# Moving one ScalarE copy (the values) ahead of four exponentials and two gelus in a fused attention and feed-forward pipeline

## The chip, the core and the metric

The kernel runs on one core of a Trainium2 chip. The core has a matrix engine (TensorE, PE in the profile; its weight loads stand apart as PEld), VectorE (DVE), ScalarE (ACT), GpSimd (POOL) and SyncE (SP), which here issues all the DMAs. Each engine works through its own instructions in the order in which they were written, and waits on semaphores for the others. The metric is the device time of one execution in microseconds (us), smaller being better. Everything is in 32-bit floats.

## The reference

The input is 4 sequences of 1024 tokens with 128 features. After a layernorm, 8 blocks of linear attention with a feed-forward part run over it (the first stage). After a second layernorm follow 6 layers of local attention with 16 heads of 64 features and windows of 32 tokens, each with a gated feed-forward part (the second stage). The change lies in the second stage, whose layer is

```
def attn_layer(x, Wqkv, qs, ksc, Wo):
    q, k, v = jnp.split(x @ Wqkv, 3, -1)          # 16 heads of 64 each
    q = l2norm(q) * qs;  k = l2norm(k) * ksc
    q = rotate(q);  k = rotate(k)                 # cos/sin tables with a scale
    out = local_attention(q, k, v)                # scores, mask, softmax, times v
    return out @ Wo                               # own window of 32 and the one before
def ffn_layer(x, g, bln, W1, b1, W2, b2):
    hg = layernorm(x, g, bln) @ W1 + b1
    a, gate = jnp.split(hg, 2, -1)                # 341 features each
    return a * jax.nn.gelu(gate, approximate=False) @ W2 + b2
for i in range(6):
    x = attn_layer(shift_tokens(x), ...) + x
    x = ffn_layer(shift_tokens(x), ...) + x
```

## The kernel before, in words

The second stage is a software pipeline over 192 tiles (6 layers of 32 tiles, 128 tokens each). Every engine has a loop `for s in range(-3, TILES + LAG)`, and each pass, here a step, does different parts of the work for different tiles: the products for tile s + 1 or s, the exponentials for tile s - 1, the product of probabilities and values for tile s - 3. The feed-forward part works on chunks of four tiles, with a lag of 8 to 11 steps, so the steps come in groups of four. In this document a group's steps are named by what the chunk does in them:

- step D (lag 8): TensorE turns the chunk (`ff_turn`), VectorE takes its statistics, ScalarE normalizes it (`ff_unit`, L974);
- step A (lag 9): TensorE turns it back (`ff_back`), ScalarE scales it (`ff_norm`, L982);
- step B (lag 10): three gate products (`ff_gate`, L783) and three value products (`ff_value`, L791) on TensorE, three gelus on ScalarE (`ff_gelu`, L988), three products `ff_hidden` on VectorE (L1278);
- step C (lag 11): TensorE's last feed-forward product (`ff_down`, L798).

In time the order is A, B, C, D, A and so on. 46 chunks have their step B in a step in which `values` runs too (the chunk's lag of 10 leaves the last two of 48 to the drain).

TensorE's order in a step is: keys (`keys_of`, L667), `attend` (L739), queries (L667), `turn_k` (L699), the chunk's turns, `output` (L748), `turn_q` (L699), `ff_down` in step C, values (`values_of`, L667), the first gate and value products in step B, `scores` (L720), the rest of the gate and value products in step B. The product of the values goes to the two banks `kv_ps`, where the keys of the next step go too: `keys_of` waits for `v_r`, which ScalarE's copy of the values (`values`, L969) counts up. `values_of` itself waits until VectorE has read the next tile's keys there. `turn_k` waits for GpSimd's `unit_k` (L497), `turn_q` for its `unit_q` (L503); between these two GpSimd does `probs_norm` (L490). All three wait for VectorE.

ScalarE's order in a step is: square of the keys (L930), `outputs` (L962), square of the queries (L930), `turned_k` (L941), eight exponentials (L954, one for each head, each with a read of its accumulator), `turned_q` (L946), four exponentials, two gelus in step B, `values` (L969), `ff_norm` in step A, `ff_unit` in step D, the third gelu in step B, the last four exponentials, and a small copy of keys (L935). Gelu and exponential are in different tables, so step B holds two loads of a table (ACT_TABLE_LOAD, 1.28 us each).

VectorE waits for the last exponential of tile s - 1 before it masks the scores of tile s (`masked`, L1240), since both use `sc`. Then come the reciprocal of the sums, the maxima, the rotation of the next keys, the transpose of the probabilities (L1255), and the rest of its step. In step B it takes the gelu's output from `gate`, a single buffer that the next gelu overwrites.

The program's order is the order written in the loops; no scheduler changes it.

Of the kernel before, what the change touches and what calls it, by code (L numbers as in the profile page):

```python
# [71 lines left out]
def build(nc, xT, wa1, wa2, wb, wf, rot, mask, outT):  # L72
    with ExitStack() as ctx:
# [129 lines left out]
        def live(t):  # L203

            return 0 <= t < TILES

        def chunk(s, lag):

            return (s - lag) // PER if (s - lag) % PER == 0 and 0 <= s - lag < TILES else None

        def need(eng, s, v):

            if v > 0:
                eng.wait_ge(s, v)
# [9 lines left out]
        def x_at(c):  # L224

            _, b, u = of(c)
            return slice(seq_col(b, COL * u), seq_col(b, COL * u) + COL)
# [300 lines left out]
        def _(pe):  # L528
# [21 lines left out]
            def first_matmul(bank, c, w, count):  # L550
                l, _, _ = of(c)
                pe.matmul(ps[:, bank, :], Wa1[l % 2][:, w * D:(w + 1) * D], X[:, x_at(c)], start=True, stop=True)\  # L552
                    .then_inc(count, 1)

            def query(c):
                l, _, _ = of(c)
                if c % NC == 0:
                    pe.wait_ge(la1[l % 2], 16 * (l // 2 + 1))
                x_in(pe, c)
                if c > 0:  # L560
                    pe.wait_ge(Q_r, c)
                first_matmul(Q_BANK, c, 0, qp_mm)
# [273 lines left out]
        def _(act):  # L836
# [51 lines left out]
            def ff_gelu(c):  # L888
                act.wait_ge(f2_mm, MA * c + 4)
                act.activation(g2[c % 2], ps[:, F2_BANK, :], ACT.Gelu_apprx_tanh, bias=vec(c, A2_BF2))\  # L890
                    .then_inc(g2_r, 1)
# [35 lines left out]
            def square(t, src, half, mm, count):  # L927
                act.wait_ge(mm, t + 1)
                need(act, red_r, t)
                act.activation(sq[:, half], src.rearrange("p b c -> p (b c)"), ACT.Square).then_inc(count, 1)  # L930

            def keys_on(t):

                need(act, s_mm, t)
                act.activation(kT[:, :, 0:WIN], kT[:, :, P:P + WIN], ACT.Copy,  # L935
                               scale=inside[:, t % TS:t % TS + 1]).then_inc(shift_r, 1)

            def turned_k(t):
                act.wait_ge(trk_mm, t + 1)
                act.wait_ge(shift_r, t + 1)  # L940
                act.activation(kT[:, :, WIN:WIN + P], s_ps.rearrange("p b (c t) -> p (b c) t", t=P),  # L941
                               ACT.Copy).then_inc(kT_r, 1)

            def turned_q(t):
                act.wait_ge(trq_mm, t + 1)
                act.activation(qTf, s_ps.rearrange("p b c -> p (b c)"), ACT.Copy).then_inc(qT_r, 1)  # L946

            def exponents(t, some):

                if some[0] == 0:  # L950
                    act.wait_ge(max_r, t + 1)
                    need(act, pt_r, t)
                for h in some:
                    i = act.activation(pe3[:, :, h, :], sc[:, 64 * h:64 * h + 64].rearrange("p (k q) -> p k q", k=2),  # L954
                                       ACT.Exp, bias=nmx[:, h:h + 1], accum_out=rs[:, h:h + 1])
                if some[-1] == HEADS - 1:
                    i.then_inc(exp_r, 1)

            def outputs(t):
                act.wait_ge(pv_mm, t + 1)  # L960
                need(act, wo_r, t)
                act.activation(OTf.rearrange("p (c r q) -> p r c q", r=2, q=WIN),  # L962
                               o_ps.rearrange("p r (c q) -> p r c q", q=WIN), ACT.Copy).then_inc(ot_r, 1)

            def values(t):

                act.wait_ge(v_mm, t + 1)
                need(act, vs_in, 32 * (t - 1))
                act.activation(vv[t % RING][:, 1, :], kv_ps.rearrange("p b c -> p (b c)"), ACT.Copy).then_inc(v_r, 1)  # L969

            def ff_unit(q):
                act.wait_ge(frs_r, 2 * q + 2)
                for j in range(PER):
                    i = act.activation(fx[:, j * P:(j + 1) * P], ps[:, FO_BANK, j * P:(j + 1) * P], ACT.Identity,  # L974
                                       bias=shift[:, j:j + 1], scale=rstd[:, 0, j:j + 1])
                i.then_inc(fn_r, 1)

            def ff_norm(q):
                if q % (NT // PER) == 0:
                    act.wait_ge(lf, 16 * (q * PER // NT + 1))  # L980
                act.wait_ge(fb_mm, q + 1)
                act.activation(fn, ps[:, FO_BANK, :], ACT.Identity, bias=WF[:, F_B:F_B + 1],  # L982
                               scale=WF[:, F_G:F_G + 1]).then_inc(xn_r, 1)
# [8 lines left out]
            for s in range(-3, TILES + LAG):  # L992
                if live(s + 1):
                    square(s + 1, kv_ps, K, k_mm, sqk_r)
                if live(s - 3):
                    outputs(s - 3)
                if live(s + 1):
                    square(s + 1, q_ps, Q, q_mm, sqq_r)
                if live(s):
                    turned_k(s)  # L1000
                if live(s - 1):
                    exponents(s - 1, range(0, 4))
                    exponents(s - 1, range(4, 8))
                if live(s):
                    turned_q(s)
                if live(s - 1):
                    exponents(s - 1, range(8, 12))
                if chunk(s, 10) is not None:
                    ff_gelu(chunk(s, 10), 0)
                    ff_gelu(chunk(s, 10), 1)  # L1010
                if live(s):
                    values(s)
                if chunk(s, 9) is not None:
                    ff_norm(chunk(s, 9))
                if chunk(s, 8) is not None:
                    ff_unit(chunk(s, 8))
                if chunk(s, 10) is not None:
                    ff_gelu(chunk(s, 10), 2)
                if live(s - 1):
                    exponents(s - 1, range(12, 16))  # L1020
                if 0 < s + 1 < TILES:
                    keys_on(s + 1)
# [380 lines left out]
```

## Time and profile before

| | us |
|---|---|
| median of 3 runs | 3965.4 (3961.76 to 3970.67) |
| the profiled execution | 3970.83 |
| its span in the profile | 3969.0 |

| engine | busy us | share of the span |
|---|---|---|
| PE (matmuls) | 3711.0 | 93% |
| DVE | 3427.1 | 86% |
| ACT | 3283.5 | 83% |
| POOL | 2394.3 | 60% |

The mean granted clock of TensorE is 0.981 of full speed. The second stage runs from about 915 us to the end, three quarters of the span. Busy time of TensorE includes time in which a matmul waits in the pipeline, so 93% doesn't say that it works at its peak. The share of an engine doesn't say either whether it is waited for: for this the waits and the order of events within a group of four steps have to be read.

### The profile page before, as it was taken

What the parts mean: (1) busy time and instruction counts of PE and PEld (TensorE: products, weight loads), DVE (VectorE), ACT (ScalarE), POOL (GpSimd) and SP (SyncE); (2) the same over time, 40 slices, a digit from 0 to 9 for tenths busy, and PEclk for the clock granted to TensorE, in tenths of its full rate; (3) what the DMA queues carried; (4) which work ended last, traced back from release to release, by engine and by line L of the source; (5) the groups of instructions that cost most, each with busy time, mean ns of one, the idle gap of its engine ahead of it and who ended that gap; (6) DMA issues with size and microseconds to landing.
All of it is one profiled execution on the core that took longest, in us unless ns stands there. A gap on an engine that the chain in (4) does not pass through costs nothing.

```text
span 3969.0 us, 124299 instructions
## 1 busy us (share of the span) xinstructions
PE 3711.0 (93%) x49248; PEld 2334.9 (59%) x49248; DVE 3427.1 (86%) x7048; ACT 3283.5 (83%) x9269; POOL 2394.3 (60%) x1468
## 2 busy tenths in 40 slices
PE   5999999976999999999999999999999999999996
PEld 2444444433666666666666666666666666666664
DVE  6999999957888988889888888988989889898894
ACT  3999999964888888888888888888888888888884
POOL 2444433435766767667676666766767667676672
PEclk7999999987999999999999999999999999999998
DMA  1000000001222323223232232322323223232321
GB/s 50 3 9 11 12 9 21 17 1 38 79 82 77 97 81 84 82 75 99 80 85 82 76 95 79 88 77 81 97 79 86 78 80 98 81 86 79 84 79 54
DMA packets 129599, 263.07 MB, mean 66 GB/s; under 512 B 34944, under 2 KB 36736, under 8 KB 128768
## 3 DMA queue, kind: packets, MB, share of 16 engines
q1 hardware_dynamic: 129024, 255.16, 23.0%
q8 instruction: 391, 6.41, 0.7%
q14 instruction: 184, 1.51, 0.1%
HBM read 26.43 MB, written 2.10 MB: 7 GB/s over the span
## 4 chain that ended last, share of the span: by engine, by line
PE 48%; ACT 23%; DVE 16%; issue 7%; POOL 4%; DMA 2%; SPq 2%; DVEq 0%; ACTq 0%; POOLq 0%
PE ps L667 12%; ACT arena L954 12%; PE ps L739 6%; PE ps L611 5%; PE ps L606 5%; PE ps L552 4%; PE ps L547 3%; ACT arena L941 3%; ACT arena L946 2%; DVE arena L1255 2%; DVE arena L1176 2%; PE ps L798 2%; DVE arena L1169 2%; DVE ssq L1197 2%; PE ps L748 2%
## 5 line engine op out<-in xcount | busy, mean ns | idle before, releaser
L954 ACT ACTIVATE arena<-arena,nmx 128x64 f32<-128x64 f32 x3072 | 1024.9, 340 | 42.3 <-DVE arena L1255 40.3
L497 POOL TENSOR_TENSOR arena<-arena,rinv 128x1024 f32<-128x1024 f32 x192 | 365.3, 1902 | 622.3 <-DVE rinv L1228 622.3
L667 PE MATMUL ps<-WB,arena 128*128 128x512 f32 x1152 | 572.4, 620 | 50.3 <-ACT arena L969 30.5
L667 PE MATMUL ps<-WN,arena 128*128 128x512 f32 x1152 | 560.1, 608 | 38.3 <-ACT arena L969 30.8
L954 ACT ACTIVATION_READ_ACCUMULATOR arena<-arena,nmx 128x1 f32 x3072 | 594.5, 194 | 0.0
L930 ACT ACTIVATE arena<-ps 128x1024 f32<-128x1024 f32 x384 | 392.1, 1021 | 227.6 <-PE ps L667 222.0
L481 POOL TENSOR_TENSOR arena<-arena 128x1024 f32<-128x1024 f32 x192 | 454.3, 2366 | 182.1 <-DVE arena L1169 162.1
L1176 DVE TENSOR_TENSOR arena<-ps,tables 128x512 f32<-128x512 f32 x768 | 490.1, 678 | 18.7 <-ACT arena L930 18.5
L486 POOL TENSOR_TENSOR arena<-arena 128x1024 f32<-128x1024 f32 x192 | 453.6, 2362 | 50.7 <-DVE arena L1169 47.1
L739 PEld LDWEIGHTS ps<-arena 128*64 128x64 f32 x12288 | 379.6, 139 | 164.2 <-issue 132.0
L1169 DVE TENSOR_TENSOR arena<-ps,tables 128x1024 f32<-128x1024 f32 x384 | 459.4, 1196 | 0.0
L1197 DVE TENSOR_REDUCE ssq<-arena 128x32 f32<-128x2048 f32 x192 | 435.2, 2267 | 0.0
L699 PEld LDWEIGHTS ps<-ident,arena 128*128 128x128 f32 x3072 | 353.8, 142 | 117.5 <-issue 102.7
L490 POOL TENSOR_TENSOR arena<-arena,rr 128x1024 f32<-128x1024 f32 x192 | 367.7, 1915 | 87.3 <-DVE rr L1249 87.3
L739 PE MATMUL ps<-arena 128*64 128x64 f32 x12288 | 405.4, 225 | 15.6 <-DMA arena<-arena 14.6
L699 PE MATMUL ps<-ident,arena 128*128 128x128 f32 x3072 | 399.9, 273 | 13.4 <-POOL arena L497 4.3
L720 PEld LDWEIGHTS ps<-arena 64*32 64x32 f32 x24576 | 265.4, 105 | 189.8 <-issue 188.2
L748 PE MATMUL ps<-arena,WB 128*128 128x128 f32 x3072 | 374.7, 275 | 2.2 <-ACT arena L962 1.1
L503 POOL TENSOR_TENSOR arena<-arena,rinv 128x1024 f32<-128x1024 f32 x192 | 370.0, 1927 | 0.0
L748 PEld LDWEIGHTS ps<-arena,WB 128*128 128x128 f32 x3072 | 358.1, 192 | 2.7 <-DMA WB<-wb 1.3
L443 POOL TENSOR_TENSOR rstdA<-veA,power 128x4 f32<-128x4 f32 x128 | 129.7, 1013 | 369.5 <-DVE veA L1129 369.5
L667 PEld LDWEIGHTS ps<-WB,arena 128*128 128x128 f32 x1152 | 202.9, 193 | 234.8 <-issue 211.9
(113 smaller groups left out, 7104.5 us busy)
## 6 DMA issues: line engine op xcount, KB each, us to landing
arena<-arena SPq DMA_DIRECT2D x1536, 64.0 KB
arena<-arena SPq DMA_DIRECT2D x192, 384.0 KB, 3.4
arena<-arena SPq DMA_DIRECT2D x192, 128.0 KB, 3.5
arena<-X SPq DMA_DIRECT2D x96, 128.0 KB, 3.1
arena<-Y SPq DMA_DIRECT2D x96, 128.0 KB, 3.1
WB<-wb SPq DMA_DIRECT2D x15, 512.0 KB, 5.8
arena<-wa SPq DMA_DIRECT2D x8, 581.0 KB, 3.7
WN<-wb SPq DMA_DIRECT2D x9, 512.0 KB, 4.6
```

The source lines that it names most:

```text
L481: pool.tensor_tensor(tu[:, K], t1[:, K], t2[:, K], ALU.add).then_inc(addk_r, 1)
L486: pool.tensor_tensor(tu[:, Q], t1[:, Q], t2[:, Q], ALU.add).then_inc(addq_r, 1)
L503: pool.tensor_tensor(heads(tu[:, Q]), heads(tu[:, Q]), wide(rinv[:, 0:HEADS], DH), ALU.mult).then_inc(q_r, 1)
L667: i = pe.matmul(banks[:, c, :], x, W[:, w * INNER + c * COL:w * INNER + (c + 1) * COL], start=True, stop=True)
L699: i = pe.transpose(s_ps[:, j // 4, (j % 4) * P:(j % 4 + 1) * P], src[:, j * P:(j + 1) * P], ident[:, :])
L739: i = pe.matmul(o_ps[64 * a:64 * a + 64, side, c * 64:(c + 1) * 64], vv[t % RING][:, side, h * DH:(h + 1) * DH], pw[:, side, :, a, c, :], ...
L748: i = pe.matmul(o_ps[:, 0, 0:P], WB[:, B_WO + c * D:B_WO + (c + 1) * D], OT[:, c, :], start=(c == 0), stop=(c == NP - 1))
L930: act.activation(sq[:, half], src.rearrange("p b c -> p (b c)"), ACT.Square).then_inc(count, 1)
L954: i = act.activation(pe3[:, :, h, :], sc[:, 64 * h:64 * h + 64].rearrange("p (k q) -> p k q", k=2), ACT.Exp, bias=nmx[:, h:h + 1], accum_o ...
L1169: dve.tensor_tensor(heads(t1[:, half]), src.rearrange("p b (h d) -> p (b h) d", d=DH), w, ALU.mult)\
L1176: k = dve.tensor_tensor(heads(t2[:, half])[:, :, here], src.rearrange("p b (h d) -> p (b h) d", d=DH)[:, :, there], w, ALU.mult)
L1197: dve.tensor_reduce(ssq[:, :], heads(sq), AX_X, ALU.add).then_inc(red_r, 1)
```

## The change

In ScalarE's loop, `values(s)` moves up by one or two places: it stood behind the third group of four exponentials and, in step B, behind two gelus. Now it stands directly behind `turned_q(s)`. Nothing else differs; the instructions, their sizes and their waits are the same.

```
                 if live(s):
                     turned_q(s)
+                    values(s)
                 if live(s - 1):
                     exponents(s - 1, range(8, 12))
                 if chunk(s, 10) is not None:
                     ff_gelu(chunk(s, 10), 0)
                     ff_gelu(chunk(s, 10), 1)
-                if live(s):
-                    values(s)
                 if chunk(s, 9) is not None:
                     ff_norm(chunk(s, 9))
```

The first place is ScalarE's step B, from `turned_q` (L946) on, before the change: the copy of the values is L969, the gelus are L988, the exponentials L954.

```order
L946 ACTIVATE arena<-ps 128x1024
L954 ACTIVATE arena,rs<-arena,nmx 128x2x32 x4
L988 ACT_TABLE_LOAD
L988 ACTIVATE arena<-ps,WF 128x512 x2
L969 ACTIVATE arena<-ps 128x1024
L988 ACTIVATE arena<-ps,WF 85x512
L954 ACT_TABLE_LOAD
L954 ACTIVATE arena,rs<-arena,nmx 128x2x32 x4
```

The same stretch of ScalarE's step B after the change.

```order
L946 ACTIVATE arena<-ps 128x1024
L969 ACTIVATE arena<-ps 128x1024
L954 ACTIVATE arena,rs<-arena,nmx 128x2x32 x4
L988 ACT_TABLE_LOAD
L988 ACTIVATE arena<-ps,WF 128x512 x2
L988 ACTIVATE arena<-ps,WF 85x512
L954 ACT_TABLE_LOAD
L954 ACTIVATE arena,rs<-arena,nmx 128x2x32 x4
```

The copy moved from between the second and the third gelu to a place ahead of the first table load, and the three gelus now follow one another.

The second place is ScalarE's step C, the one with no chunk work on this engine, from `turned_q` (L946) to the copy of keys (L935), before the change.

```order
L946 ACTIVATE arena<-ps 128x1024
L954 ACTIVATE arena,rs<-arena,nmx 128x2x32 x4
L969 ACTIVATE arena<-ps 128x1024
L954 ACTIVATE arena,rs<-arena,nmx 128x2x32 x4
L935 ACTIVATE arena<-arena,inside 128x8x32
```

The same stretch of step C after the change.

```order
L946 ACTIVATE arena<-ps 128x1024
L969 ACTIVATE arena<-ps 128x1024
L954 ACTIVATE arena,rs<-arena,nmx 128x2x32 x8
L935 ACTIVATE arena<-arena,inside 128x8x32
```

All eight of the remaining exponentials now stand behind the copy, where four stood before. The order on the other four engines is the same.

## Rows read from the trace of the kernel before

**Rows 1.** Waits of PE from 1000 to 3800 us: us in total, times, longest.

```profile
PE ps L667 <- ACT arena L969: 59.4, 90, 0.8
PE ps L783 <- ACT arena L988: 5.7, 35, 0.4
```

**Rows 2.** Waits of DVE from 1000 to 3800 us.

```profile
DVE arena L1278 <- ACT arena L988: 141.7, 82, 3.2
```

**Rows 3.** Timeline, step B: start, us, engine, line, xcount, [idle before <-releaser].

```profile
2017.58 1.01 ACT L946 ACTIVATE arena<-ps 128x1024 f32<-128x1024 f32 x1
...
2019.93 1.28 ACT L988 ACT_TABLE_LOAD   x1
...
2021.22 0.69 ACT L988 ACTIVATE arena<-ps,WF 128x512 f32<-128x512 f32 x1
2021.94 0.75 DVE L1278 SCALAR_TENSOR_TENSOR arena<-ps,WF,arena 128x512 f32<-128x512 f32 x1 [2.35 <-ACT arena L988]
...
2022.79 0.69 ACT L988 ACTIVATE arena<-ps,WF 128x512 f32<-128x512 f32 x1 [0.88 <-DVE arena L1278]
2023.37 1.02 ACT L969 ACTIVATE arena<-ps 128x1024 f32<-128x1024 f32 x1
...
2023.53 1.09 PE L783 MATMUL ps<-arena,WF 128*85 128x512 f32 x2 [0.16 <-ACT arena L988]
...
2024.66 0.68 ACT L988 ACTIVATE arena<-ps,WF 85x512 f32<-85x512 f32 x1 [0.27 <-PE ps L783]
...
2025.31 1.88 PE L667 MATMUL ps<-WB,arena 128*128 128x512 f32 x4
```

**Rows 4.** Timeline, the step C behind it.

```profile
2035.78 1.00 ACT L946 ACTIVATE arena<-ps 128x1024 f32<-128x1024 f32 x1
...
2037.07 1.88 PE L667 MATMUL ps<-WB,arena 128*128 128x512 f32 x4
...
2038.99 1.02 ACT L969 ACTIVATE arena<-ps 128x1024 f32<-128x1024 f32 x1 [0.88 <-PE ps L667]
...
2039.91 0.34 ACT L954 ACTIVATE arena<-arena,nmx 128x64 f32<-128x64 f32 x1
...
2041.23 0.50 ACT L935 ACTIVATE arena<-arena,inside 128x256 f32<-128x256 f32 x1
...
2041.43 1.22 DVE L1240 TENSOR_TENSOR arena<-ps,maskt 128x1024 f32<-128x1024 f32 x1
```

**Rows 5.** Busy time from C's masking to A's values: window, us, then each engine.

```profile
2041.43:2065.25 23.82, 23.06 (x350) 16.66 (x349) 23.09 (x41) 20.30 (x65) 19.38 (x11) 1.00 0.39 110
```

**Rows 6.** Timeline, the end of step D and step A.

```profile
2052.95 1.01 ACT L969 ACTIVATE arena<-ps 128x1024 f32<-128x1024 f32 x1
...
2053.86 1.49 ACT L974 ACTIVATE arena<-ps,shift,rstd 128x128 f32<-128x128 f32 x4
...
2054.11 1.96 PE L667 MATMUL ps<-WB,arena 128*128 128x512 f32 x4 [0.76 <-ACT arena L969]
...
2055.99 1.95 PEld L739 LDWEIGHTS ps<-arena 128*64 128x64 f32 x64 [0.76 <-ACT arena L974]
...
2056.84 1.90 POOL L497 TENSOR_TENSOR arena<-arena,rinv 128x1024 f32<-128x1024 f32 x1 [1.92 <-DVE rinv L1228]
...
2058.70 1.92 POOL L490 TENSOR_TENSOR arena<-arena,rr 128x1024 f32<-128x1024 f32 x1
...
2060.57 1.91 POOL L503 TENSOR_TENSOR arena<-arena,rinv 128x1024 f32<-128x1024 f32 x1
...
2062.82 0.91 PEld L699 LDWEIGHTS ps<-ident,arena 128*128 128x128 f32 x8
```

**Rows 7.** Timeline, from step A into an earlier step B.

```profile
2007.19 1.95 PE L667 MATMUL ps<-WB,arena 128*128 128x512 f32 x4 [0.68 <-ACT arena L969]
...
2012.50 1.91 POOL L503 TENSOR_TENSOR arena<-arena,rinv 128x1024 f32<-128x1024 f32 x1
...
2015.46 0.91 PEld L699 LDWEIGHTS ps<-ident,arena 128*128 128x128 f32 x8
```

More of the change, by code:

```diff
@@ L1005, in _ @@
                     turned_q(s)
+                    values(s)
                 if live(s - 1):
@@ L1010, in _ @@
                     ff_gelu(chunk(s, 10), 1)
-                if live(s):
-                    values(s)
                 if chunk(s, 9) is not None:
```

## The prediction

> **What bounds the kernel now.** I read the page's busy shares first (TensorE 93%, VectorE 86%, ScalarE 83%: no engine is far from full), then the waits of TensorE and VectorE, and then one whole group of four steps in the timeline, because the waits alone don't tell what is late next. The waits show the target of this change: over 2800 us TensorE stands still 90 times for the copy of the values, 59.4 us in all, 0.66 us a time [rows 1]. 2800 us hold about 45 groups, so it is two of the four steps. The timeline says which: the keys at the start of A (0.76 us, behind D) and at the start of B (0.68 us, behind A) [rows 6, 7]. Behind B and C the keys start without such a wait [rows 3]. The second thing to see is who else is near the edge. In step B VectorE idles 2.35 us for the first gelu, and TensorE starts its third gate product as soon as the second gelu ends, 0.16 us after it could have [rows 3]; over the whole stage TensorE waits there 35 times, but only 5.7 us [rows 1], so the two are level. From C's masking to A's values VectorE is busy 23.09 of 23.82 us, and TensorE 23.06 [rows 5]: two engines that run side by side, neither with room. VectorE's slack all lies in B, where it waits for gelus 141.7 us in all [rows 2].
>
> **The change, part by part.** No instruction is added or removed, so the working is in the places. The copy takes 0.91 us of ScalarE's queue (from its start at 2052.95 to the next instruction at 2053.86 [rows 6]). All is for one group of four steps, relative to before, positive being later.
>
> Steps D and A, the gain. The copy no longer stands behind four exponentials. D's turned queries end about 0.2 us before the product of the values is there, so the copy would run about 1 us earlier, and end before TensorE has finished the scores. Both waits of the keys go: up to 0.76 + 0.68 = 1.44 us a group, if nothing else is late.
>
> Step B, the first loss. ScalarE runs without a gap from the turned queries (2017.58) into the table load and the first gelu (2021.22) [rows 3]. The copy now stands in this chain, and its product is done by then, so that it doesn't wait: every gelu comes 0.91 us later. Before, the copy lay in a hole: between the second gelu and the third, ScalarE has to wait for TensorE's third gate product anyway, and even with the copy in it 0.27 us of that hole was left [rows 3]. So the cover is free and goes unused. The third gate product starts when the second gelu ends, the next keys behind it, and VectorE's three products wait for the gelus too. The slack is nil on TensorE (it already waits 0.16 us), and VectorE's idle 2.35 us grow instead of shrinking. TensorE and VectorE both enter C 0.91 us late.
>
> Step C, the second loss. Between the turned queries and the values TensorE does `ff_down` here. The turned queries end at 2036.78, the product of the values only lets ScalarE go on at 2038.99 [rows 4]. Before, four exponentials filled 1.32 us of this and 0.88 us were idle; now 2.2 us are idle, and the four exponentials come behind the copy. Four of them take 2041.23 - 2039.91 = 1.32 us [rows 4]. Queued behind the waiting copy are these, the last four, the copy of keys and the next square. VectorE's masking waits for the last exponential; it started at 2041.43 without a wait, some 0.10 us after that exponential, so it now starts 1.32 - 0.10 = 1.22 us later. VectorE is then 0.91 + 1.22 = 2.13 us late, TensorE 0.91. ScalarE itself has idle time soon after, and catches up.
>
> Steps D and A, what is late next. VectorE has no room here [rows 5], so it stays 2.13 us late; and it feeds GpSimd. In A, `unit_k` waits for VectorE, with `probs_norm` and `unit_q` right behind it [rows 6], so all three are 2.13 us late, and `unit_q` ends at 2060.57 + 1.91 + 2.13 = 2064.61. TensorE wanted to turn these queries at 2062.82 [rows 6]. It turns them 1.79 us late, whatever it gained at the start of A. Nor was all of that gain there: `attend` in A waits for ScalarE's `ff_unit`, 2055.99 [rows 6], which stands behind copy and exponentials as before and is 0.65 us late by the same working. From the turn to the scores all is 1.79 us late. The keys of B then start without their 0.68 us: 1.79 - 0.68 = 1.11 us a group later than before.
>
> Does it settle there? B's keys are 1.11 us late and VectorE 2.13, 1.02 us behind TensorE. In B `unit_q` ended at 2014.41 and the turn of the queries came at 2015.46 [rows 7]: 1.05 us of slack, which just holds 1.02. The 2.35 us in front of the first gelu then take up VectorE's lag, and the next group starts as this one did. So the loss is 1.11 us in each group.
>
> Other queues: SyncE shifts the values behind their copy, and waits for it (the eight issues for the probabilities, in front of it, are out by then), and the shifted values are used three steps later. The transposed probabilities of D are 2.1 us later, their DMAs too; by their issues in the trace they would land about a microsecond ahead of the `attend` that needs them. The table loads stay two a group, at 1.28 us [rows 3].
>
> **The sum.** 46 groups x 1.11 us = 51 us. The profiled execution took 3970.8 us, so its like would take 4022; it lay 5.4 us above the median of the runs, and against that median of 3965.4 the forecast is 4016 us, 1.3% slower. The parts not seen in a row are small: the 0.1 us between last exponential and masking could be 0 to 0.2; how far VectorE recovers between C and A is bounded by 0 and its idle 23.82 - 23.09 = 0.73 us [rows 5]. That gives 0.4 to 1.2 us a group, 3984 to 4021. Upwards, if DMAs or the 1.02 against 1.05 us of slack in B add up to 0.6 us, 4044.
>
> **The rivals.**
> 1. Both waits go and nothing comes back: 1.44 us x 46 = 66 us less, 3899. For it speaks only the list of waits, in which the copy is TensorE's largest wait for another engine [rows 1]. It would need slack behind the copy in B, and there is none [rows 3]. The Trainium skill (Perfetto Trace Analysis, Optimization Strategies) says that where the matmul engine is idle waiting for others, one should optimize the engines that block it; taken alone, this rule gives that time.
> 2. Faster, the other side: B costs its 0.91 us, both waits go, and VectorE's lag from C never reaches TensorE: 0.91 - 1.44 = -0.53 us x 46, 3941. The place is `unit_q` in A: it ends at 2062.48, 0.34 us before TensorE's turn [rows 6]. Faster comes out if VectorE is less than about 0.9 us late there; I have 2.13.
> 3. No change: C costs nothing (the masking isn't held), all engines carry B's 0.91 us, and A gains only down to `ff_unit`: 0.65 late at `attend`, less 0.68 at B's keys, nil. 3966.
> 4. Worse: the lags add up with nothing taken back, 0.91 + 1.22 = 2.13 us x 46 = 98 us, 4063. It would need the keys to keep waiting for their copy, which now comes about 1 us earlier.
>
> **How the numbers follow.** A measurement here tells 0.2%, about 8 us, from no change. Chances: forecast 0.71, rival 1 0.03, rival 2 0.09, rival 3 0.08, rival 4 0.09. Faster 0.12 (rivals 1 and 2), same 0.08, slower 0.80. The range from 3980 to 4050 holds the forecast's own spread and half of what lies between it and rival 4; the faster cases and rival 3 stay outside.
>
> **What would show it.** Right: TensorE's wait for the copy nearly gone; ScalarE's wait for the product of the values in front of L969 grown from 0.88 to 2.2 us in C; VectorE's wait for the gelus grown to above 3 us in B; TensorE's wait at the third gate product 0.9 us or more; a new wait of TensorE's turn for GpSimd's L503 in A; the group of four steps 1.1 us longer. Wrong: the masking in C at its old place relative to the keys (rival 3), or TensorE's turn in A without a wait for L503 (rival 2). What would upset all of it is a copy that waits long in B.

## The result and the profile after

| | before | after |
|---|---|---|
| median of the runs, us | 3966.6 (4 runs) | 4033.9 (4 runs, 4031.4 to 4037.8) |
| ratio of after to before | | 1.017 (95% interval 1.0157 to 1.0182) |
| span of the profiled execution, us | 3969.0 | 4034.4 |
| busy us PE, DVE, ACT, POOL | 3711.0, 3427.1, 3283.5, 2394.3 | 3730.8, 3424.8, 3283.4, 2395.2 |

The change makes the kernel slower by 67 us; forecast were 51, with a range of 3980 to 4050. The work of the engines is the same (ScalarE's busy time differs by 0.1 us); what grew is waiting. In the kernel after, VectorE's lines stand one lower: L1239 is the masking, L1254 the transpose, L1277 the product with the gate.

The waits of TensorE from 1000 to 3860 us (total, times, longest), to be held against [rows 1]:

```profile
PE ps L739 <- DMA arena<-arena: 49.6, 66, 1.3
PE ps L720 <- ACT arena L946: 22.6, 46, 0.8
PE ps L791 <- ACT arena L988: 19.5, 39, 0.6
PE ps L783 <- ACT arena L988: 19.5, 44, 0.7
...
PE ps L699 <- POOL arena L503: 11.8, 35, 0.8
```

The wait for the copy, 59.4 us before, is gone altogether. Five others are now large, 123 us together, where they were about 21 before. Two are for the gelus of step B, one is for GpSimd's `unit_q` in step A, as forecast. The first two, put down to DMAs and to the turned queries, were not.

The first row has to be taken apart before it can be used. `attend` waits for several things: the DMAs of its tile's probabilities, the DMAs that shift its tile's values (done 13 us before in the group below), VectorE's sum `Y` of the tile before, and in step A also ScalarE's `ff_unit`. The list names whichever of their semaphores moved last, even if the count that `attend` asks for had been reached long before. In step A of the group shown below (in the kernel after):

```profile
2070.25 0.59 SPq L354 DMA_DIRECT2D arena<-arena  x1
...
2072.36 1.48 ACT L974 ACTIVATE arena<-ps,shift,rstd 128x128 f32<-128x128 f32 x4
...
2073.84 0.27 DVE L1259 TENSOR_TENSOR Y<-ps,X 128x128 f32<-128x128 f32 x1
...
2074.38 2.08 PE L739 MATMUL ps<-arena 128*64 128x64 f32 x64 [0.81 <-DMA arena<-arena]
```

The last probability DMA landed 0.50 us before `attend` started, by its semaphore. VectorE's `Y` ended at 2074.11, 0.27 us before it, and this is what came last. The DMA that the row names is the shift of a later tile's values. Held against the counts that `attend` asks for, the row splits like this in each trace (us, times, 1000 to 3800 us; the rows for this window are within 0.1 us of the sums):

| | the tile's probability DMAs last (nearly all in step B) | `ff_unit` or `Y` last (all in step A) |
|---|---|---|
| before | 4.5, 13 | none |
| after | 21.4, 30 | 28.3, 36 |
| D and A early (e1 below) | 19.8, 29 | 14.1, 27 |
| D early (e10) | 4.0, 13 | 14.9, 28 |
| A early (e11) | 19.1, 26 | none |
| e1 with half of the DMAs (e6) | none | 16.2, 29 |
| after with half of the DMAs (e7) | none | 36.0, 38 |

So the DMAs really hold `attend` for 21 us after the change, not for 49.6. The part in step A was seen in the forecast, which named `ff_unit` for it; the part in step B was not.

Step B after the change in the timeline (start, us, engine, line, [idle before <-releaser]), against [rows 3]:

```profile
2038.10 1.28 ACT L988 ACT_TABLE_LOAD   x1
2039.40 0.69 ACT L988 ACTIVATE arena<-ps,WF 128x512 f32<-128x512 f32 x1
2040.12 0.75 DVE L1277 SCALAR_TENSOR_TENSOR arena<-ps,WF,arena 128x512 f32<-128x512 f32 x1 [3.01 <-ACT arena L988]
2040.14 1.12 PE L791 MATMUL ps<-arena,WF 128*128 128x512 f32 x2 [0.55 <-ACT arena L988]
2040.96 0.69 ACT L988 ACTIVATE arena<-ps,WF 128x512 f32<-128x512 f32 x1 [0.88 <-DVE arena L1277]
2041.70 1.09 PE L783 MATMUL ps<-arena,WF 128*85 128x512 f32 x2 [0.44 <-ACT arena L988]
2042.83 0.68 ACT L988 ACTIVATE arena<-ps,WF 85x512 f32<-85x512 f32 x1 [1.18 <-PE ps L783]
```

ScalarE's idle time before the third gelu grew from 0.27 to 1.18 us: by 0.91 us, the length of the copy that lay there. VectorE's wait for the first gelu grew from 2.35 to 3.01 us. TensorE's wait at the third gate product is 0.44 us, where 0.9 or more was forecast, since 0.55 us of it now fall on the second value product (L791), which also needs the first gelu. The two make 0.99 us.

From step C to the next step B, against [rows 4, 6, 7]:

```profile
2057.17 1.02 ACT L969 ACTIVATE arena<-ps 128x1024 f32<-128x1024 f32 x1 [2.21 <-PE ps L667]
2060.93 1.23 DVE L1239 TENSOR_TENSOR arena<-ps,maskt 128x1024 f32<-128x1024 f32 x1 [1.38 <-ACT arena L954]
...
2076.09 1.90 POOL L497 TENSOR_TENSOR arena<-arena,rinv 128x1024 f32<-128x1024 f32 x1 [1.92 <-DVE rinv L1227]
...
2081.23 0.35 ACT L954 ACTIVATE arena<-arena,nmx 128x64 f32<-128x64 f32 x1 [0.89 <-DVE arena L1254]
2081.77 1.09 PE L699 MATMUL ps<-ident,arena 128*128 128x128 f32 x8 [0.30 <-POOL arena L503]
...
2085.04 1.59 PE L720 MATMUL ps<-arena 64*32 64x64 f32 x128 [0.46 <-ACT arena L946]
2086.57 1.98 PE L667 MATMUL ps<-WB,arena 128*128 128x512 f32 x4
2089.03 2.09 PE L739 MATMUL ps<-arena 128*64 128x64 f32 x64 [0.48 <-DMA arena<-arena]
```

All of this is read against the first gelu of the group (2021.22 before, 2039.40 after). The copy in C waits 2.21 us, forecast 2.2. The masking comes 21.53 us behind the gelu, before 20.21: 1.32 us later, forecast 1.22. In A, `unit_k` is 1.07 us later, so VectorE made up 0.25 us on the way. TensorE turns the queries late and waits for GpSimd, as forecast. But ScalarE's exponentials in A now wait 0.89 us for VectorE's transpose, because they overwrite what it reads, so that the turned queries are late too, and the scores with them. Then B's `attend` waits 0.48 us for its DMAs, and here they do land last, 0.14 us before it starts.

How long is one group? The table load ahead of the first gelu marks each. In nearly every trace several groups have the same length within 0.03 us, which is also the shortest; these are the undisturbed ones. (The group of the timeline above is 62.68 us long, 0.56 above it, and 0.48 of this is B's wait for DMAs.) One before the change, from one such row to the next:

```profile
2582.86 1.28 ACT L988 ACT_TABLE_LOAD   x1
...
2643.71 1.28 ACT L988 ACT_TABLE_LOAD   x1
```

and after it:

```profile
2548.31 1.28 ACT L988 ACT_TABLE_LOAD   x1
...
2610.43 1.28 ACT L988 ACT_TABLE_LOAD   x1
```

60.85 against 62.12 us: 1.27 us a group, against 1.11 in the forecast. In the mean over 46 groups it is 67 / 46 = 1.46 us. The 46 lengths of each trace tell where: the 40 ordinary groups grew by 1.51 us in the mean, the five that hold a boundary of layers by 0.65, and the last, in the drain, by 1.67.

### The profile page after: what moved, and what is told of

Same layout as the page of the kernel before. It is cut to its first block, busy times and chain, and to the rows that moved or that the text cites. A ratio compares the mean times of both kernels' runs of the same rounds, so it can differ in the third digit from the quotient of the medians.

```text
span 4034.4 us, 124299 instructions
## 1 busy us (share of the span) xinstructions
PE 3730.8 (92%) x49248; PEld 2341.1 (58%) x49248; DVE 3424.8 (85%) x7048; ACT 3283.4 (81%) x9269; POOL 2395.2 (59%) x1468
## 3 DMA queue, kind: packets, MB, share of 16 engines
q14 instruction: 184, 1.51, 0.1%
## 4 chain that ended last, share of the span: by engine, by line
PE 47%; DVE 19%; ACT 17%; issue 7%; POOL 5%; SPq 3%; DMA 2%; DVEq 0%; ACTq 0%; POOLq 0%
PE ps L667 11%; ACT arena L954 8%; PE ps L611 5%; PE ps L739 5%; PE ps L606 5%; PE ps L552 4%; PE ps L547 3%; DVE arena L1175 3%; PE ps L798 3%; DVE arena L1254 3%; DVE arena L1168 2%; PE ps L748 2%; PE ps L699 2%; DVE ssq L1196 2%; ACT arena L969 2%
## 5 line engine op out<-in xcount | busy, mean ns | idle before, releaser
L954 ACT ACTIVATE arena<-arena,nmx 128x64 f32<-128x64 f32 x3072 | 1023.7, 339 | 72.6 <-DVE arena L1254 71.5
L954 ACT ACTIVATION_READ_ACCUMULATOR arena<-arena,nmx 128x1 f32 x3072 | 589.8, 192 | 0.0
L739 PEld LDWEIGHTS ps<-arena 128*64 128x64 f32 x12288 | 381.9, 139 | 214.7 <-issue 138.1
L739 PE MATMUL ps<-arena 128*64 128x64 f32 x12288 | 406.6, 225 | 62.9 <-DMA arena<-arena 61.9
L720 PEld LDWEIGHTS ps<-arena 64*32 64x32 f32 x24576 | 268.7, 105 | 204.6 <-issue 202.6
L503 POOL TENSOR_TENSOR arena<-arena,rinv 128x1024 f32<-128x1024 f32 x192 | 369.9, 1927 | 0.0
L1239 DVE TENSOR_TENSOR arena<-ps,maskt 128x1024 f32<-128x1024 f32 x192 | 234.9, 1223 | 149.2 <-ACT arena L954 140.3
```

The lines of the kernel that those rows point to most:

```text
L503: pool.tensor_tensor(heads(tu[:, Q]), heads(tu[:, Q]), wide(rinv[:, 0:HEADS], DH), ALU.mult).then_inc(q_r, 1)
L739: i = pe.matmul(o_ps[64 * a:64 * a + 64, side, c * 64:(c + 1) * 64], vv[t % RING][:, side, h * DH:(h + 1) * DH], pw[:, side, :, a, c, :], ...
```

## The experiments

Each ratio is to the kernel before, run on the same chip. In the kernels e1 to e4 and e8 to e12 the copy stands early in the steps that are named, and elsewhere as before. The edit of e1 is

```
                 if live(s):
                     turned_q(s)
+                if live(s) and s % 4 in (0, 1):
+                    values(s)
...
-                if live(s):
+                if live(s) and s % 4 not in (0, 1):
                     values(s)
```

where s % 4 is 0 in D, 1 in A, 2 in B and 3 in C. The others have another set: (0, 1, 2) for e2, (0, 1, 3) for e3, (3,) for e8, (2,) for e9, (0,) for e10, (1,) for e11.

**e1: D and A alone.**

> The copy of the values moves ahead only in steps D and A; B and C keep the old order. My theory: the two waits of TensorE for the copy vanish (1.44 us a group), but the gain is cut by what is level with them in the trace of before: in A the first exponentials wait for VectorE's transpose, which ends as the turned keys do, and the attend of B waits for DMAs that follow that transpose. What is left is 0.1 to 0.7 us a group, taken as 0.5: 46 x 0.5 = 23 us, 3943 us, ratio 0.994. Rival (the waits are worth what the list says): 1.44 x 46 = 66 us less, 3900. Rival (VectorE and its DMAs close the loop by themselves): 0.1 x 46, about 3961, no change.

Measured: 3957.7 us, ratio 0.9974 (0.9965 to 0.9984), so some 10 us or 0.22 us a group, of the 1.44 us in the list of waits. The rival that takes the list at its word is refuted. The sign and the cause of the cut are those of the theory, at the lower part of its 0.1 to 0.7 us. Where the waits went is plain in TensorE's waits from 1000 to 3800 us:

```profile
PE ps L739 <- DMA arena<-arena: 33.9, 56, 1.6
PE ps L720 <- ACT arena L946: 23.2, 48, 0.8
```

The 59.4 us of waits for the copy are down to 4.3, and these two rows have grown by 44.2 us together (before: 4.4 and 8.5). Of the 33.9 us, 19.8 are for the DMAs, nearly all in step B, and 14.1 are in step A, for `ff_unit` and `Y`. A row of its own, `PE ps L739 <- ACT arena L974`, holds another 5.0 us of that.

**e2: D, A and B (C as before).**

> As in the changed kernel, but step C keeps the old order, so that the four exponentials stand ahead of the copy there. My theory: B costs its 0.91 us, C nothing, D and A give about 0.5 us: +0.4 us a group, 46 x 0.4 = 18 us, 3985 us, ratio 1.005; VectorE's masking in C starts where it did before, relative to the gelus; TensorE's waits for DMAs and for GpSimd's L503 are gone again. Rival (C costs nothing, the whole loss is B's): as the changed kernel, 4034, 1.017. Rival (the saved waits count in full): 0.91 - 1.44, 3942.

Measured: 3996.6 us, ratio 1.0062 (1.0045 to 1.0079). The forecast for it was 1.005. C's order does cost something, and B's too: beside e1, B's early copy costs 0.0088, 35 us. In an undisturbed group the masking in C comes 21.51 us behind the table load, as before the change (22.83 in the kernel after), and the waits for L503 are back at 1.9 us (1.5 before), both as expected. The row of waits for DMAs isn't gone, as expected it would be, but 32.2 us.

**e3: D, A and C (B as before).**

> As in the changed kernel, but step B keeps the old order, with the copy between the second and the third gelu. My theory: B's 0.91 us go and all else stays as in the changed kernel: 1.46 - 0.91 = 0.55 us a group, 46 x 0.55 = 25 us, 3992 us, ratio 1.006; VectorE's wait for the gelus is back near 3.2 us a group, masking in C is 1.3 us late after the gelus. Rival (C costs nothing): as with D and A alone, 3943.

Measured: 3993.0 us, ratio 1.0063 (1.0046 to 1.0080), as forecast. Beside e1, C's early copy costs 35 us as well. VectorE's wait for the gelus (same stretch) is back near that of before (141.7), while its wait for exponentials stays as high as in the changed kernel (81.3 before, 128.3 after):

```profile
DVE arena L1242 <- ACT arena L954: 127.8, 132, 1.8
DVE arena L1280 <- ACT arena L988: 124.9, 75, 3.2
```

**e4: D and A early, and in B the copy between the first and the second gelu.**

```
                     ff_gelu(chunk(s, 10), 0)
+                    if live(s):
+                        values(s)
                     ff_gelu(chunk(s, 10), 1)
...
+                if live(s) and s % 4 not in (0, 1) and chunk(s, 10) is None:
+                    values(s)
```

> D and A as in e1, C old; in B the copy stands between the first and the second gelu, where ScalarE idles 0.88 us for VectorE anyway. My theory: the copy's 0.91 us fill that hole and delay the second gelu by 0.03 us, so the time is that of e1 within 0.05 us a group (2 us). Rival (any place ahead of the last gelu delays the gelu chain by the copy's 0.91 us): 42 us above e1.

Measured: 3953.9 us, ratio 0.9966 (0.9953 to 0.9978), the same as e1 within the intervals. So it isn't being ahead of a gelu that costs: in this place the copy replaces ScalarE's wait for VectorE, which falls from 41.8 us in e1 to 7.3 us. The wait ahead of the third gelu, where the copy used to lie, grows from 10.4 to 46.0 us, and costs nothing, since TensorE sets that time:

```profile
ACT arena L988 <- PE ps L783: 46.0, 39, 1.2
...
ACT arena L988 <- DVE arena L1282: 7.3, 5, 1.6
```

**e5, e6, e7: half of the DMAs.** Of the eight DMAs a tile, the four for the previous window are not issued, and the counts that wait for them are halved:

```
                     sp.dma_start(PTw[q, w % 2, here], pt[q, COL:2 * COL]).then_inc(wide_in, 16)
-                    sp.dma_start(PTw[o:o + WIN, w % 2, here], pt[q, 0:COL]).then_inc(wide_in, 16)
...
-                pe.wait_ge(wide_in, 32 * PARTS * (t + 1))
+                pe.wait_ge(wide_in, 16 * PARTS * (t + 1))
```

e5 is the kernel before with this edit.

> The kernel before, but of the eight DMAs that spread the transposed probabilities of a tile only the four for the own window are issued; the four that carry the previous window's probabilities are left out, so that part of the attention output is missing. SyncE's issues per tile fall from some 5.0 us to 2.5 us. My theory: TensorE waits for these DMAs only 4.4 us in the whole stage of the kernel before, so no more than about 4 us are to be had: 3962, ratio 0.999. Rival (the DMAs load the memories and slow everything): clearly faster than that.

Measured: 3958.5 us, ratio 0.9973 (0.9963 to 0.9984), 10 us less, more than the 4 us expected. The lengths of the groups say where it is. An undisturbed group is as long as before, 60.85 us, so the DMAs don't slow every group. (They do lengthen one product in it by 0.1 us, see e7, but in the kernel before TensorE waits for the copy behind that product anyway, and this wait grew from 59.4 to 66.7 us.) The 45 full groups together are 4.5 us shorter, which is the wait of 4.4 us in the list. The last group, in the drain, is another 3.5 us shorter (47.88 to 44.35 us). It lies behind the 3800 us at which the list ends: in it TensorE waits 10.2 us for DMAs in the kernel before, and in e5 none, but 6.3 us for ScalarE and VectorE. That is 8 of the 10 us; the other 2 are within the spread of executions.

e6 is the kernel of e1 with it.

> The kernel of e1 (copy early in D and A only) with the same four DMAs left out. My theory: in e1 the saved waits for the copy turned into waits of attend for these DMAs (33.9 us), and of the scores for the turned queries. With the DMAs out of the way the keys' 0.68 us in B get through to the gelus: 46 x 0.68 = 31 us less than the kernel with half the DMAs and the old order, about 3932, ratio 0.9915 to the kernel before. Rival (the DMAs only fill time that VectorE or ScalarE would take anyway): no faster than e1, 3956.

Measured: 3931.2 us, ratio 0.9907 (0.9891 to 0.9924), as forecast. The early copy in D and A is worth 10 us with all DMAs and 27 us (0.9973 to 0.9907) with half of them. So the DMAs were what took most of the gain. An undisturbed group is 60.07 us long, 0.78 less than in e5. TensorE's real waits for these DMAs fell from 19.8 us to nothing; what the list still puts down to DMAs, 16.2 us, is `attend` in step A waiting for `ff_unit` and `Y` (in this kernel's file the line numbers are lower by one):

```profile
PE ps L719 <- ACT arena L945: 20.1, 43, 0.8
PE ps L738 <- DMA arena<-arena: 16.2, 29, 1.0
```

e7 is the changed kernel with it.

> The changed kernel with the same four DMAs left out. My theory: its groups without a DMA wait take 62.12 us against 60.85 before, 1.27 us more, so the DMAs' part of the 1.46 us a group is 0.19 us: 46 x 0.19 = 9 us less, 4025, ratio 1.015. Rival (all of its 49.6 us of waits for DMAs count): 3984, ratio 1.005.

Measured: 4005.9 us, ratio 1.0101 (1.0084 to 1.0118), between my 4025 and the rival's 3984. The DMAs cost the changed kernel about 28 us, and 10 of these the kernel before as well, so 18 of the 67 us are theirs, near the 17 us by which the real waits for them grew (4.5 to 21.4). My 9 us was too little, since it took the change of an undisturbed group for the whole of what isn't the DMAs'. The rival took all of the row of 49.6 us for DMAs, and 28 us of that aren't. In this kernel `attend` in step A still waits 0.94 us in a row that names a DMA, with the last of the four issues over 6 us back:

```profile
1299.77 2.41 SPq L353 DMA_DIRECT2D arena<-arena  x4
...
1307.82 0.27 DVE L1258 TENSOR_TENSOR Y<-ps,X 128x128 f32<-128x128 f32 x1
...
1308.35 2.08 PE L738 MATMUL ps<-arena 128*64 128x64 f32 x64 [0.94 <-DMA arena<-arena]
```

An undisturbed group takes 62.02 us, 1.17 more than in e5. The 0.10 us below the 62.12 of the kernel after lie in A's scores (L720), which take 1.57 us there and 1.47 here. In all eleven kernels with eight DMAs a tile A's scores take 1.58 to 1.60 us in the median, and in the three with four DMAs 1.47 or 1.48. In A the eight issues go on while the scores are made. In B and C they are over by then, and the scores take 1.48 or 1.49 us in every trace. So the scores are 0.1 us longer where they meet these DMAs; how that comes about isn't shown.

**e8: C alone.**

> The copy moves ahead in step C alone; A, B and D keep the old order. My theory: masking in C is 1.3 us late after the gelus, VectorE's transpose in A about 1.07 us late, ScalarE's first exponentials wait for that transpose, and since the copy in A stands behind them, the keys of B are late by the same: 46 x 1.0 = 46 us, 4012, ratio 1.0116. Rival (the cost of C is the 0.75 us a group by which e3 and e1 differ): 4001, ratio 1.0088. Rival (C costs nothing, only the order in B does): 3966.

Measured: 4002.8 us, ratio 1.0089 (1.0072 to 1.0106), so the time is the first rival's, 35 us. But the mechanism is the theory's; an undisturbed group takes 61.92 us, 1.07 more than before, as it said, and its masking in C comes 22.83 us behind the table load, as in the kernel after.

What was wrong is the multiplier, in two ways. The five groups that hold a boundary of layers are as long as before: 65.93 to 66.03 us, against 65.93 to 66.59 in the kernel before. And the 40 ordinary ones grew by 0.92 us in the mean, since some were longer than 60.85 us before and the delay is in part hidden there. So 1.07 us times 46 is too much, and the mean is 0.76.

**e9: B alone.**

> The copy moves ahead in step B alone. My theory: every group's gelus, third gate product and next keys come 0.91 us later, and nothing else changes: 46 x 0.91 = 42 us, 4009, ratio 1.0106. Rival (it costs what it cost beside the early copies of D and A, e2 less e1, 0.76 us a group, since some groups hide it): 4002, ratio 1.0089. Rival (the copy is hidden somewhere in B): 3967.

Measured: 4008.7 us, ratio 1.0105 (1.009 to 1.0121), as forecast, and undisturbed groups take 0.92 us more (61.77). Nearly all groups pay here, those at a boundary too (66.85 to 67.08 us).

**e10, e11, e12: which wait was worth anything.**

> The copy moves ahead in step D alone, which takes away the wait of 0.76 us at the keys of A. My theory: nothing comes of it, since A's attend waits for the normalized chunk, its turned queries for GpSimd, and its exponentials for VectorE's transpose, all at their old times; and the copy in A, behind these exponentials, holds the keys of B as before: 3967, ratio 1.000 within 0.001. Rival (each of the two waits gives half of what e1 gave): ratio 0.9987. Rival (the wait counts in full): 46 x 0.76 = 35 us less, 0.991.

> The copy moves ahead in step A alone, which takes away the wait of 0.68 us at the keys of B. My theory: all of what e1 gained comes from here, so 3957, ratio 0.9974. Rival (half each): 0.9987.

> As e11, and in B the copy stands between the first and the second gelu as in e4. A candidate for the best order: the copy early only where TensorE's wait for it matters, and elsewhere in ScalarE's idle time. My theory: as e11 within 2 us, 3956, ratio 0.997.

Measured:

| | ratio | 95% interval | us |
|---|---|---|---|
| e10, D alone | 1.0006 | 0.9997 to 1.0015 | 3967.7 |
| e11, A alone | 0.9975 | 0.9966 to 0.9984 | 3956.8 |
| e12, A, and B between the gelus | 0.9974 | 0.9963 to 0.9985 | 3957.6 |

All three as forecast. The larger wait of the two, 0.76 us at the keys of A, is worth nothing; all of e1's gain comes from the smaller one, at the keys of B. TensorE's waits in e10 show the exchange (1000 to 3800 us). Of the 59.4 us, 27.8 left, and came back in the next two rows, where 8.5 and 4.4 us stood before:

```profile
PE ps L667 <- ACT arena L969: 31.6, 51, 0.8
PE ps L720 <- ACT arena L946: 21.2, 45, 0.8
PE ps L739 <- DMA arena<-arena: 18.8, 40, 1.0
```

Of the last row, 14.9 us are in step A: `attend` waits there for `ff_unit` (and sometimes `Y`), as expected, and not for its DMAs. In e11 it is the other way round: all 19.1 us are B's `attend` waiting for the DMAs of its probabilities.

The best complete kernel is e1, e4, e11 or e12, which can't be told from one another: 0.25% to 0.34% under the kernel before.

**All in one measure.** The shortest full group in each trace (us) is repeated within some 0.03 us, while the times of whole executions spread by several us. The change to the kernel before, with all DMAs:

| copy early in | shortest group | change |
|---|---|---|
| none (before) | 60.84 | |
| D (e10) | 60.87 | +0.03 |
| A (e11) | 60.15 | -0.69 |
| B (e9) | 61.75 | +0.91 |
| C (e8) | 61.91 | +1.07 |
| D, A (e1) | 60.16 | -0.68 |
| D, A, B (e2) | 61.08 | +0.24 |
| D, A, C (e3) | 61.20 | +0.36 |
| all four (after) | 62.10 | +1.26 |

The four single steps add up to 1.32 us, against 1.26 for all of them, and D, A and B to 0.25 against 0.24.

## Why the prediction was right, and where its sizes were off

Right, and shown:

- The two waits for the copy go, and in A nothing comes of it, while in B an undisturbed group gains 0.69 us (e11), as "without their 0.68 us" says. In the list of waits they were 59.4 us; alone (e1) they bring 10, which puts rival 1 out.
- Step B: the copy in the gelu chain costs its own length. Forecast 0.91 us a group; e9 measured 0.92 in an undisturbed group, and 42 us in all. Of the signs for it one failed: 0.44 us in place of 0.9 at the third gate product, with 0.55 more ahead of the second value product. e4 shows that it is the place in the chain, not the order in itself.
- Step C: the copy waits 2.21 us for a product that stands behind `ff_down`, and VectorE's masking comes 1.32 us later (forecast 1.22). That this delay reaches TensorE, against rivals 2 and 3, is shown by e8: C alone costs 35 us.
- Rival 4 (2.13 us a group, 4063) is out: the copy's waits are gone and the undisturbed group is 1.27 us longer, not 2.13.

Off in size: the term "1.11 us a group later", times 46.

- For an undisturbed group it is 1.27 us. The term that was too small is "from the turn to the scores all is 1.79 us late": the scores don't wait for the turned queries' product alone but for ScalarE's copy of it, behind eight exponentials that wait for VectorE's transpose. In the group of the timeline the scores come 45.64 us behind the gelu against 44.58 before (2065.80 in the trace of before), 1.06 us later; the forecast came to 1.79 - 0.91 = 0.88. In the trace of before the transpose and the turned keys ended together in step A, which the prediction didn't look at. The 0.25 us that VectorE made up worked the other way: the turn itself comes only 0.66 us later behind the gelu (2081.77, against 2062.93 before), not 0.88.
- The 0.65 us by which A's `attend` was to be late, behind `ff_unit`, was too small as well, and the engine was the wrong one. It starts 1.1 us later than before (0.21 us later behind the gelu), and what it waits for last is VectorE's `Y`. This didn't reach the sum, since the turn waits for `unit_q` anyway.
- The DMAs of the transposed probabilities were weighed only for D, where they seemed a microsecond ahead, and there they are indeed no limit (`attend` in A waits for them once, 0.6 us). Those of A, needed by B's `attend`, were put at nothing. e7 and e5 together put them at 18 us, and the real waits at 17.
- Against this, groups at a layer boundary hide C's delay (e8), and ordinary groups that were longer than 60.85 us before hide part of it, so that not all 46 pay it in full. These two partly cancel, which is luck: 46 groups at 1.27 us make 58 us, the DMAs bring some 17 more, and the hidden part, as what is left of the 67, takes some 8 off. So the sum lies 16 us above the forecast.

In whole executions the parts don't add up quite: e9 alone is 42 us and e8 alone 35, together 77 without the gain of 10 from D and A, so 67. That is the measured loss, but in company with the early copies of D and A each costs 35, which would make 60. These differences of a few us are near what the intervals allow (4 to 7 us each). In undisturbed groups the parts do add up, so the rest lies in the groups that are longer; which of their waits make it up is open.

## What to carry to other kernels

When two engines run side by side without room, a wait in the list is worth only the distance to the next thing that is late. Before moving a producer earlier, write down for each step what else would release the waiting engine, and by how much it is earlier; here it was 0.1 us or less for one wait of 0.76. Where the waiting instruction has several conditions, look up which of them was met last, since the list may name another: more than half of a row of 49.6 us was not the DMAs'. And where a loop is steady, compare the length of its undisturbed rounds, which tells 0.03 us where the time of the whole doesn't tell 0.2 us a round. And a moved instruction does harm where it leaves an idle hole of its engine for a busy chain: a copy in an in-order queue belongs into the gap where that engine waits anyway, which can be a different place in each step of the same loop.
